# A weight statistic's loads move to another queue, and a layer norm's small operations are batched over all tokens

## What is computed

```python
def attn(x): ...   # q, k, v projections, rope, causal softmax, Wo
def _weight_quant(w):
    scale = jnp.clip(jnp.mean(jnp.abs(w)), EPS, None)
    return jnp.clip(jnp.round(w / scale), -1.0, 1.0) * scale
def _act_quant(x):
    scale = 127.0 / jnp.clip(jnp.max(jnp.abs(x), axis=-1, keepdims=True), EPS, None)
    return jnp.clip(jnp.round(x * scale), -128.0, 127.0) / scale
def _bitlinear(x, w):
    return jnp.einsum('...i,oi->...o', _act_quant(x), _weight_quant(w))
def ffn(x):
    gate, up = _bitlinear(x, w_gate), _bitlinear(x, w_up)
    return _bitlinear(jax.nn.silu(gate) * up, w_down)
x = x + attn(_layernorm(x))
x = x + ffn(_layernorm(x))
```

## Time and profile before

| | us |
|---|---|
| median of 2 runs | 11149.96 (11145.91 to 11154.02) |
| profiled execution | 11138.1 |
| its span, slowest core (core 1) | 11136.5 |
| fastest core (core 7) | 11090.6 |
| busy: TensorE matmul / VectorE / ScalarE / GpSimd | 6011.1 / 4176.4 / 2392.6 / 1242.4 |

### The profile page before, as it was taken

The page is one execution under the profiler, slowest core; times in us unless marked ns, Lnnn a source line. Parts: engine busy times, 40 slices in busy tenths (PEclk is TensorE's granted clock), DMA queues, the critical chain, the costliest instruction groups (busy, mean ns, idle before and its releaser), DMA issues.

```text
span 11136.5 us, 92492 instructions; the slowest of 8 cores (11090.6 to 11136.5 us)
## 1 busy us (share of the span) xinstructions
PE 6011.1 (54%) x23698; PEld 2263.0 (20%) x23698; DVE 4176.4 (38%) x5066; ACT 2392.6 (21%) x4196; POOL 1242.4 (11%) x587
## 2 busy tenths in 40 slices
PE   0016564975554555556222218888877855363727
PEld 0002222431111101111000003333333322121313
DVE  3423233132222222222233327777777752415050
ACT  4441011003343434334223310000000010101010
POOL 0002122000000000000000013333333300000000
PEclk9999898987777767677666659999999977686858
DMA  3251422421111011110444444334334423333433
GB/s 106 91 132 40 78 48 53 86 68 32 59 32 60 32 60 40 52 60 23 134 151 156 156 138 128 123 126 127 123 123 128 127 67 119 104 127 94 136 95 130
DMA packets 632549, 1048.44 MB, mean 94 GB/s; under 512 B 338930, under 2 KB 420850, under 8 KB 570354
## 3 DMA queue, kind: packets, MB, share of 16 engines
q1 hardware_dynamic: 455268, 656.55, 19.6%
q10 hardware_dynamic: 168192, 352.40, 9.1%
q0 software_dynamic: 8592, 33.59, 1.8%
HBM read 807.51 MB, written 218.10 MB: 92 GB/s over the span
## 4 chain that ended last, share of the span: by engine, by line
DVE 30%; PE 27%; ACT 12%; issue 9%; DMA 7%; POOL 6%; ACTq 3%; SPq 3%; DVEq 1%; another core or an unknown queue 1%; POOLq 0%
PE pb L68 21%; DVE p_cu L68 4%; ACT p_E L68 3%; PE p2S L68 3%; DVE p_hqt L68 3%; ACTq L68 3%; SPq L68 3%; ACT p_dump L68 2%; POOL p_wdtb L68 2%; DVE p_pm L68 2%; DVE p_wf L68 2%; DVE p_invr L68 2%; DVE p_ht L68 2%; POOL k_pp_t L68 1%; ACT wa_dump L68 1%
## 5 line engine op out<-in xcount | busy, mean ns | idle before, releaser
L68 PE MATMUL pb<-p_wgt,p_xiT 128*128 128x512 bf16 x4096 | 1078.6, 424 | 613.2 <-DVE p_ht L68 434.4
L68 PE MATMUL pb<-p_wds,p_hTg 128*128 128x512 bf16 x4096 | 921.0, 389 | 272.3 <-DMA p_wds<-wdtd 272.2
L68 ACT ACTIVATE p_E<-pb,p_negB 128x512 bf16<-128x512 f32 x1280 | 879.8, 687 | 777.8 <-PE pb L68 621.4
L68 PE MATMUL p2S<-p_E,g_ones_colb 128*1 128x512 bf16 x1280 | 534.8, 418 | 501.9 <-DVE p_E L68 274.1
L68 DVE TENSOR_TENSOR p_cu<-g_sxinv,p4a_swn 128x1 f32<-128x1 f32 x256 | 767.0, 2996 | 27.9 <-DVE p_cg L68 1.5
L68 DVE TENSOR_TENSOR p_E<-p_E,p_masks 128x512 bf16<-128x512 bf16 x512 | 218.1, 426 | 1477.6 <-ACT p_E L68 1477.2
L68 PE MATMUL pb<-p_Wo,p_ct 128*128 128x512 bf16 x1024 | 259.3, 421 | 859.5 <-DMA p_ct<-ctxTd 726.5
L68 PEld LDWEIGHTS pb<-p_wgt,p_xiT 128*128 128x128 bf16 x4096 | 427.3, 107 | 1246.8 <-issue 887.4
L68 ACT ACTIVATE p_sg<-pb,p_cg 128x512 f32<-128x512 f32 x256 | 175.9, 687 | 2194.1 <-DVE p_cu L68 1309.5
L68 PE MATMUL pb<-k_pp_xT,k_pp_W 128*128 128x512 bf16 x2048 | 467.1, 383 | 298.1 <-ACT k_pp_qb L68 195.3
L68 PEld LDWEIGHTS pb<-p_wds,p_hTg 128*128 128x128 bf16 x4096 | 406.9, 100 | 785.6 <-issue 327.8
(11 more groups left out here) (159 smaller groups left out, 6740.8 us busy)
## 6 DMA issues: line engine op xcount, KB each, us to landing
p_wds<-wdtd ACTq DMA_DIRECT2D x128, 1024.0 KB, 5.7
wa_t<-wgT SPq DMA_DIRECT2D x64, 1024.0 KB, 6.8
wa_t<-wuT SPq DMA_DIRECT2D x64, 1024.0 KB, 5.9
wa_t<-wdT SPq DMA_DIRECT2D x64, 1024.0 KB, 5.0
p_wf<-wdT SPq DMA_DIRECT2D x64, 1024.0 KB, 6.3
p_wf<-wgT SPq DMA_DIRECT2D x64, 1024.0 KB, 5.9
p_wf<-wuT SPq DMA_DIRECT2D x64, 1024.0 KB, 5.4
hfpd<-p_ht ACTq DMA_DIRECT2D x256, 256.0 KB, 3.1
```

The lines of the kernel that those rows point to most:

```text
L68: real = getattr(eng, meth)(*a, **k)
```

## The change

- `wa_chunk` waits and issues on `G` (GpSimd) instead of `Y` (SyncE).
- `wa_feed` takes 6 chunks a head instead of 5. In the output projection it takes 4 a block in the first loop and 2 a block in the second, where it was 7 a block.
- The projection is split in two loops. The first makes `x1b`, stores it and takes its sum, sum of squares, max and min into column tb of four 128x16 tiles `sw_`. Then the small operations are done once on 128x16. The second loop loads `x1b` back from `d_x1`, quantizes and stores `d_xint`.
- `x1rel[sl]` is now a list: the store's semaphore, ScalarE's and VectorE's last reads. An unused tile `qgb` goes.

```diff
-        wait(Y, wa_state["rel"][slw])
-        sem.inc(Y.dma_start(wa_tile[slw][:, :W], wd.ap()[r0:r0 + 128, c0:c0 + W]), 16)
+        wait(G, wa_state["rel"][slw])
+        sem.inc(G.dma_start(wa_tile[slw][:, :W], wd.ap()[r0:r0 + 128, c0:c0 + W]), 16)
...
-            wa_feed(5)
+            wa_feed(6)
...
-        st3 = [sb3(f"p3_s{i}", [128, 1], F32) for i in range(10)]
+        NTB = OWN // 128
+        sw_ = [sb3(f"p3_sw{i}", [128, NTB], F32) for i in range(8)]
...
             x1sem[sl].inc(Sc.dma_start(d_x1.ap()[tb * 128:(tb + 1) * 128, :], x1b[sl][:]), 16)
-            x1rel[sl] = (x1sem[sl], x1sem[sl].v)
             wait(Sc, (sV, x1tok))
             sop("activation", dump3[:], x1b[sl][:], AF.Identity,
-                accum_out=st3[0][:])
+                accum_out=sw_[0][:, tb:tb + 1])
             wait(Sc, (sS, sS.v))
             sop("activation", dump3[:], x1b[sl][:], AF.Square,
-                accum_out=st3[1][:])
+                accum_out=sw_[1][:, tb:tb + 1])
             wait(V, (sV, sV.v), (sS, sS.v))
-            vop("tensor_reduce", st3[2][:], x1b[sl][:], AX.X, ALU.max)
+            vop("tensor_reduce", sw_[2][:, tb:tb + 1], x1b[sl][:], AX.X, ALU.max)
             wait(V, (sV, sV.v))
-            vop("tensor_reduce", st3[3][:], x1b[sl][:], AX.X, ALU.min)
...
+            vop("tensor_reduce", sw_[3][:, tb:tb + 1], x1b[sl][:], AX.X, ALU.min)
+            x1rel[sl] = [(x1sem[sl], x1sem[sl].v), (sS, sS.v), (sV, sV.v)]
+            wa_feed(4)
+        wait(V, (sV, sV.v), (sS, sS.v))
+        vop("tensor_scalar", sw_[4][:], sw_[0][:], 1.0 / 2048.0, None, ALU.mult)
...
+        vop("tensor_scalar", g_sxinv[:, 0:NTB], sw_[2][:], g_rec127[:], None,
+            ALU.mult)
+        vop("reciprocal", sw_[5][:], g_sxinv[:, 0:NTB])
...
+        stattok = (sV, sV.v)
+        wait(Y, (x1sem[0], x1sem[0].v), (x1sem[1], x1sem[1].v),
+             (sS, sS.v), (sV, sV.v))
+        x1crel = [(sV, 0), (sV, 0)]
+        for tb in range(NTB):
+            sl = tb % 2
+            wait(Y, x1crel[sl])
+            xin[sl].inc(Y.dma_start(x1b[sl][:], d_x1.ap()[tb * 128:(tb + 1) * 128, :]), 16)
+            wait(V, (xin[sl], xin[sl].v), (sV, sV.v), stattok)
+            vop("tensor_scalar", tqb[:], x1b[sl][:], sw_[6][:, tb:tb + 1],
+                sw_[7][:, tb:tb + 1], ALU.mult, ALU.add)
             vop("tensor_copy", qib[:], tqb[:])
             vop("tensor_tensor", tqb[:], tqb[:], qib[:], ALU.subtract)
             vop("tensor_scalar", tqb[:], tqb[:], MAGIC, -MAGIC, ALU.add, ALU.add)
             wait(V, xirel[sl])
             vop("tensor_tensor", xib[sl][:], qib[:], tqb[:], ALU.add)
+            x1crel[sl] = (sV, sV.v)
             wait(Sc, (sV, sV.v))
             xisem[sl].inc(Sc.dma_start(d_xint.ap()[tb * 128:(tb + 1) * 128, :],
                                        xib[sl][:]), 16)
             xirel[sl] = (xisem[sl], xisem[sl].v)
-            wa_feed(7)
+            wa_feed(2)
         wa_feed(len(wa_items))
```

More of the change, by code:

```diff
@@ L808, in build_program @@
         qib = sb3("p3_qi", [128, D], I32)
-        qgb = sb3("p3_qg", [128, D], F32)
         xib = [sb3(f"p3_xi{i}", [128, D], BF16) for i in range(2)]
-        st3 = [sb3(f"p3_s{i}", [128, 1], F32) for i in range(10)]
+        NTB = OWN // 128
+        sw_ = [sb3(f"p3_sw{i}", [128, NTB], F32) for i in range(8)]
         dump3 = sb3("p3_dump", [128, D], F32)
@@ L825, in build_program @@
         xinrel = [(sV, 0), (sV, 0)]
-        x1rel = [(dm["st0"], 0), (dm["st1"], 0)]
+        x1rel = [[(dm["st0"], 0)], [(dm["st1"], 0)]]
         xirel = [(dm["q0"], 0), (dm["q1"], 0)]
@@ L829, in build_program @@
         xisem = [dm["q0"], dm["q1"]]
-        for tb in range(OWN // 128):
+        for tb in range(NTB):
             sl = tb % 2
@@ L848, in build_program @@
                 wait(V, (sT, sT.v), (xin[sl], xin[sl].v), (sV, sV.v),
-                     x1rel[sl] if dmc == 0 else (sV, 0))
+                     *(x1rel[sl] if dmc == 0 else []))
                 vop("tensor_tensor", x1b[sl][:, dmc * 512:(dmc + 1) * 512],
@@ new lines, in build_program @@
+        vop("tensor_tensor", sw_[5][:], sw_[4][:], sw_[4][:], ALU.mult)
+        vop("tensor_scalar", sw_[6][:], sw_[1][:], 1.0 / 2048.0, None, ALU.mult)
+        vop("tensor_tensor", sw_[6][:], sw_[6][:], sw_[5][:], ALU.subtract)
+        vop("tensor_scalar", sw_[6][:], sw_[6][:], 1e-5, None, ALU.add)
+        wait(Sc, (sV, sV.v))
+        sop("activation", sw_[6][:], sw_[6][:], AF.Ln)
+        wait(Sc, (sS, sS.v))
+        sop("activation", sw_[6][:], sw_[6][:], AF.Exp, bias=0.0, scale=-0.5)
@@ new lines, in build_program @@
+        wait(V, (sS, sS.v))
+        vop("tensor_tensor", sw_[2][:], sw_[2][:], sw_[4][:], ALU.subtract)
+        vop("tensor_tensor", sw_[3][:], sw_[4][:], sw_[3][:], ALU.subtract)
+        vop("tensor_tensor", sw_[2][:], sw_[2][:], sw_[3][:], ALU.max)
+        vop("tensor_tensor", sw_[2][:], sw_[2][:], sw_[6][:], ALU.mult)
+        vop("tensor_scalar", sw_[2][:], sw_[2][:], 1e-5, None, ALU.max)
+        vop("tensor_scalar", g_sxinv[:, 0:NTB], sw_[2][:], g_rec127[:], None,
+            ALU.mult)
@@ new lines, in build_program @@
+        vop("reciprocal", sw_[5][:], g_sxinv[:, 0:NTB])
+        vop("tensor_tensor", sw_[6][:], sw_[6][:], sw_[5][:], ALU.mult)
+        vop("tensor_tensor", sw_[7][:], sw_[4][:], sw_[6][:], ALU.mult)
+        vop("tensor_scalar", sw_[7][:], sw_[7][:], -1.0, None, ALU.mult)
+        stattok = (sV, sV.v)
+        wait(Y, (x1sem[0], x1sem[0].v), (x1sem[1], x1sem[1].v),
+             (sS, sS.v), (sV, sV.v))
+        x1crel = [(sV, 0), (sV, 0)]
+        for tb in range(NTB):
+            sl = tb % 2
[4 more added lines that the diff above has]
+                sw_[7][:, tb:tb + 1], ALU.mult, ALU.add)
```

## The result

| | before | after |
|---|---|---|
| median, us (runs) | 11153.15 (10 runs, 11145.91 to 11228.67) | 10526.72 (11 runs, 10460.57 to 10543.61) |
| profiled execution, its span | 11138.1, 11136.5 | 10461.8, 10460.2 (core 2) |
| attention, first head's load to the projection's first load | 2914.6 (2421.1 to 5335.7) | 2733.2 (2424.8 to 5158.0) |
| output projection, to `g_hamax`'s memset | 1157.1 (5335.7 to 6492.8) | 647.2 (5158.0 to 5805.1) |
| mean of the eight cores: span / attention / projection | 11113.3 / 2894.0 / 1157.0 | 10443.8 / 2736.6 / 643.9 |

The ratio is 0.941 with a 95% interval of 0.939 to 0.944: 5.9% faster. The forecast was 10432 us, in a range of 10350 to 10670. The profiled execution was forecast at 10420.6 and took 41 us more (0.4%); the median lies 0.9% above its forecast.

The account below looks back on a forecast made before the run. Chains, not load, bound it: p_ct and head loads queue behind wa_tile loads. Projection 571.5 us less, attention 157 less, 11 lost: 717.5 off 11138.1 gives 10420.6, times 1.00106 a median of 10432 us, range 10350 to 10670.

Parts of the forecast that it names:

- the two stalls: Projection: TensorE waits some 52 us each for p_ct; attention: VectorE waits 21.2 us each for p_kT; both behind wa_tile loads.
- the 10.6 us taken over from the earlier trace: Attention borders: p_kT lands 10.6 us after the first issue, plus 1; VectorE's wait becomes 10 us, from 21.2.
- the 11 of heads 14 and 15: Attention, behind heads 14 and 15: no norm covers six chunks, 25.2 us for 19.9, costing 5.3 us twice.
- L: Time from a wa_tile load's issue on the GpSimd queue to its landing; taken as 8 us, bounds 5.4 and 11.5.
- Rival 5: All GpSimd-queue loads slow: L over 20.5 us, about 11373 us, chance 0.03; L 14.8 to 20.5, within 2%, 0.03.
- First loop: Projection's first loop: the two slots decide, 2 x (L + 2.1), 20.2 us a block; fifteen periods, 303.0 us.
- the bytes' (17.9): Projection's first loop: DMA bound of 17.9 us a block, weights, p_xq and p_x at 422 GB/s plus p_ct.
- Second loop and tail: Projection: chunks set 10.1 us a block (L + 2.1), 160.3 us; then store's issue and last two chunks, 5.5.
- Rival 1: Second loop: GpSimd's issue waits for VectorE, 2.6 us at most; 39 us more, 10471 us; chance 0.15.
- Rival 2: Projection and attention: the DMA engines are the bound, L reaches 11.5; 233 us more, 10665 us; chance 0.10.
- Rival 3: First loop: TensorE stays at 1.2 GHz, 27.3 us a block; 107 us more, 10539 us; chance 0.06.
- Rival 4: First loop: the overlap doesn't come about, 37.8 us a block; 264 us more, 10696 us; chance 0.02.

## Why the prediction held, and where it was off

**What bounds the kernel, and the two stalls.** Right. The profiled execution fell by 676.3 us where 717.5 were forecast. Between the two slowest cores (1 before, 2 after) attention fell by 181.5 us, the projection by 509.9, and the rest grew by 15. But the cores of one execution differ by more than these errors: attention takes 2877 to 2915 us in before, and the feed-forward stages, which nothing changes, 4627 to 4655 in after. On the mean of the eight cores the span fell by 669.5 us: attention 157 (146 forecast), the projection 513 (571.5 forecast, to an end 1.4 us earlier), the stages ahead 4 more, feed-forward 2.5 less. So attention came as forecast, and what is missing is missing in the projection.

**Attention: 157 us for 146, of two errors that cancel.** p_kT was given 11.6 us from the first issue and landed so that `normB` started after 7.4. The term that failed is the 10.6 us taken over from the earlier trace rows, with its "1 us more because chunks load beside it". In before three chunk loads were issued right ahead of it; at the new border both slots are full and no chunk is loading. (With chunk loads close to it again, in the run with all chunks in attention, the wait is 9.4 us.) VectorE's wait is 95.1 us in 14 on core 2, 6.8 each against 10 forecast:

```profile
DVE p_dump L68 <- DMA p_kT<-kTd: 95.1, 14, 8.0
```

On the mean of the cores the 14 waits fell from 277.9 to 85.3 us: 13.8 saved per border and not 11.2, 193 us and not 157. Against it stands a term that was put at nothing: the chunks hold ScalarE when the Ln's input is there. Over the 14 borders that costs 17 us on core 2 and 11 to 39 on the others, 25 on the mean; in the run with the queue alone, with five chunks a head, the Ln waits at most 0.15 us a border (five cores read), and with three slots it waits 0.6 us in all on the core read. With the 11 of heads 14 and 15 (forecast, not measured) that is 193 - 25 - 11 = 157 us, what was measured. That the sum came near was luck: 36 us more gained and 25 more lost. That ScalarE's chunks would be covered up to L = 9.6 was computed against the later Ln. With the earlier p_kT the chunks (to 3341.64, t0 + 27.2) decide already against a Ln ready at 25.9, as the timeline shows; their own end was forecast at 27.4.

**L, the landing from GpSimd.** 8 forecast; 6.1 and 5.5 at the median in attention (sync queue before: 6.6), 7.8 and 8.6 in the first loop, 9.4 in the second. The DMA issues of the first loop:

```profile
wa_t<-wdT POOLq DMA_DIRECT2D x31, 1024.0 KB, 7.8
wa_t<-wuT POOLq DMA_DIRECT2D x30, 1024.0 KB, 8.6
x1d<-p_x ACTq DMA_DIRECT2D x15, 1024.0 KB, 10.9
p_xq<-xq SPq DMA_DIRECT2D x13, 1024.0 KB, 8.6
p_ct<-ctxTd SPq DMA_DIRECT2D x13, 512.0 KB, 14.4
```

p_ct, 5.0 us in the earlier trace rows, takes 14.4 and is still early. Rival 5 (a slow queue) is out: from ScalarE the same load lands in 8.0 and 8.8. What grows from stage to stage is the load on the DMA engines, share 0.17, 0.92 and 0.81.

**First loop: 20.2 forecast, 22.4 measured** (the reduce behind the first block's statistics starts at 5245.2, that behind the last's at 5581.6: 336.4 / 15), 33 us in all. The formula 2 x (L + release) held; both its terms were short. The release was taken as 2.1 us from the sync queue; from GpSimd it is 2.55 (3316.72 to 3319.27), and L was 8.2: 21.5. The last us I put to the chunk that comes behind the statistics (argued, not tested). ScalarE in one block:

```profile
5360.81 1.91 ACT L68 ACTIVATE wa_dump<-wa_t 128x2048 f32<-128x2048 f32 x1 [2.45 <-DMA wa_t<-wuT]
...
5364.91 1.91 ACT L68 ACTIVATE wa_dump<-wa_t 128x2048 f32<-128x2048 f32 x1 [1.71 <-DMA wa_t<-wuT]
...
5370.15 1.91 ACT L68 ACTIVATE wa_dump<-wa_t 128x2048 f32<-128x2048 f32 x1 [2.85 <-DMA wa_t<-wuT]
...
5375.02 1.91 ACT L68 ACTIVATE wa_dump<-wa_t 128x2048 f32<-128x2048 f32 x1 [2.48 <-DMA wa_t<-wuT]
...
5377.95 1.91 ACT L68 ACTIVATE p_dump<-p_x 128x2048 f32<-128x2048 f32 x1 [0.54 <-ACT wa_acc L68]
```

The two slots with their latency and the bytes lie within 2 us of one another, which is why no single experiment on one of them gave much: 20.6 us with a third slot, 21.9 without GpSimd, 20.2 with half the bytes, and 16.8 with the chunks gone. The prediction's bound that was wrong by most is the bytes' (17.9): 422 GB/s is what the engines reach in a burst of 4 us with loads of the sync queue alone, not what they hold here.

**The small terms.** Wo and the first block 82.3 (76.0 forecast); the last chunks 19.3 (20.2); the batched statistics 5.1 (6.0), their 128x16 operations at 0.17 to 0.18 us where 128x1 took 0.15; the first bare reload 5.1 (5.4). The epilogue, 7.7, was as before.

**Second loop and tail: 10.1 us a block and 5.5 forecast, 10.8 and 18.4 measured**, 11 and 13 us more. It is one mis-sized term. L + release is 9.4 + 2.55 = 12.0 us here, not 10.1, and this is what the chunks take: of the two in a block the first starts at 5681.58, 5693.98 and so on to 5766.89, 12.2 us apart. VectorE ran ahead of them, at 9.0 us a block at first and up to 11.2 later, where it waited for a reload of x1 (11.7 us in 6), until its two `p_xi` tiles were full. Their stores are issued by ScalarE, behind a chunk that waits for its load, so from 5706 us on VectorE is tied to the chunks' 12 us:

```profile
5681.58 1.91 ACT L68 ACTIVATE wa_dump<-wa_t 128x2048 f32<-128x2048 f32 x1 [5.67 <-DMA wa_t<-wdT]
...
5683.74 0.34 ACTq L68 DMA_DIRECT2D xintd<-p_xi  x1
5684.14 1.55 POOL L68 DMA_DIRECT2D wa_t<-wdT  x1 [7.53 <-ACT wa_acc L68]
5684.22 1.35 DVE L68 TENSOR_SCALAR p_tq<-p_x,p_sw 128x2048 f32<-128x2048 f32 x1 [2.35 <-DMA p_x<-x1d]
...
5691.69 2.29 DVE L68 TENSOR_TENSOR p_xi<-p_qi,p_tq 128x2048 bf16<-128x2048 int32 x1 [1.06 <-DMA xintd<-p_xi]
```

When VectorE is through, the chunks that are left still take their own time, to 5795.8: the tail. The prediction summed the second loop as if ScalarE came level with VectorE at its end. It is the old fault on another queue: a store behind a wait that doesn't concern it. With all chunks gone from the stage, VectorE's block is 9.05 us and the tail is gone.

**Rival 1, the issue that waits for VectorE.** The POOL line above shows it: an issue of 0.53 us took 1.55 and ended at 5685.69, 0.12 us after VectorE's TENSOR_SCALAR (5685.57). In the first loop, where VectorE runs TENSOR_TENSOR and reduces, no issue is stretched; in the second, 9 of 31 are, by 3.6 us in all. By the Trainium skill's rule (SBUF — State Buffer, the "DVE blocks DMA" trap) this is what should happen, and the trace agrees. The price was up to 2.6 us an issue in the rival and 0.12 in the trace (3.6 us in 31): an issue rarely falls on such an operation, and the next one, a CAST, did not hold it a second time.

**Rivals 2 to 4.** Rival 2, bytes, is half right: its bound is real, at 20.6 us and not at 27.2. Rival 3 fell in the half-matmul run; the granted clock in the first loop's matmuls was 0.78 on average, and did not matter. Rival 4 fell: 22.4 us is far from 37.8 (its 15.3 us of chunks are 15.1 by the terms used, which changes nothing).

The projection, 647.2 us on core 2 for 584.2 forecast, is where the forecast was off: 33 us in the first loop, 24 in the second with its tail, 6 ahead of them. The factor from the profiled execution to the median was 1.00106, from two times of before; in after it is 1.0062, and no term of the sum has to do with it (below).

## What to carry to other kernels

A wait issued on an engine's stream is a wait for everything behind it, its unrelated loads and stores too; list what stands behind it before reading any busy share. When a stall goes, price the next bounds with rates and latencies under the new load (here 8.2 us and about 300 GB/s), not with those of the sparse kernel, and expect several bounds within 10% of one another. Then ask whether the work has to be in that stage at all: moving the chunks to where DMA was 17% busy was worth 144 us of projection (647.2 to 503.2), more than any repair of their slots.
